# A graph layer with gated mixing: the gate's first layer moves from the prologue into the main loop, and inputs arrive laid out

## The reference

```python
x = x + gnn(xn, edges) + mix(xn)          # 106250 edges, sorted by target
x = x + ffn(layernorm(x))
# gnn: h = xn @ W in 4 heads; softmax over each target's edges of
#      leaky_relu(a_src[src] + a_dst[dst]); sum of alpha * h[src]; + bias; sigmoid
# mix: q, k, v = xn @ Wqkv; context = softmax(k, over nodes)^T v; out = q @ context
#      gate = sigmoid(gelu(ln(xn) @ Wg1 + bg1) @ Wg2 + bg2)     Wg1 is 256 x 64
#      (out * gate) @ Wproj + bproj
# ffn: half of the nodes, the best by a router score, get gelu(y @ w1 + b1) @ w2 + b2
```

## Time and profile before

| | |
|---|---|
| Median of three runs | 1600.1 us (1594.01 to 1605.51) |
| Span of the profiled execution | 1323.1 us |
| The profiled execution's own time | not given; the median is 277.0 us above the span |
| TensorE matmul, weight load busy | 1060.3 us (80%), 791.9 us (60%) |
| VectorE, ScalarE, GpSimd busy | 1018.3 us (77%), 516.7 us (39%), 854.3 us (65%) |
| Mean granted TensorE clock | 0.878 |
| Main block begins at | 136.8 us |

### The profile page before, as it was taken

How to read it: one execution, slowest core, us unless ns; L and a number is a source line. 1 busy time by engine, 2 the same in 40 slices (tenths; PEclk the granted TensorE clock), 3 DMA queues, 4 the chain that set the end, 5 groups by cost and what they waited for, 6 DMA issues and landing times.

```text
span 1323.1 us, 24146 instructions
## 1 busy us (share of the span) xinstructions
PE 1060.3 (80%) x5817; PEld 791.9 (60%) x5817; DVE 1018.3 (77%) x2596; ACT 516.7 (39%) x1155; POOL 854.3 (65%) x891
## 2 busy tenths in 40 slices
PE   5998857785687878878788787897877978779786
PEld 4674635553465566656666566675665766567565
DVE  6776365657788877888788887888878878888788
ACT  4462423212334434343353443434434334344421
POOL 0621656767777777777777777777777777777000
PEclk9999878886788889888898888988889888898889
DMA  9527556766666666666666666666666666665205
GB/s 269 136 72 141 155 184 179 191 178 166 161 173 166 164 160 165 176 158 166 169 162 174 165 161 176 158 171 164 164 173 161 168 164 166 175 164 151 68 1 195
DMA packets 165907, 212.04 MB, mean 160 GB/s; under 512 B 49524, under 2 KB 131252, under 8 KB 165704
## 3 DMA queue, kind: packets, MB, share of 16 engines
q0 software_dynamic: 39984, 110.94, 33.8%
q1 hardware_dynamic: 117570, 97.15, 25.6%
q10 hardware_dynamic: 8306, 3.41, 1.2%
HBM read 165.93 MB, written 45.46 MB: 160 GB/s over the span
## 4 chain that ended last, share of the span: by engine, by line
PE 50%; DVE 15%; issue 11%; ACT 7%; DMA 3%; SPq 1%; DVEq 1%; ACTq 0%; POOL 0%; POOLq 0%
PE bank L1922 15%; PE bank L1887 14%; PE bank L1859 6%; PE bank L1898 5%; ACT L1630 4%; PE bank L1838 3%; DVE hot L1272 2%; PE bank L1847 2%; PE bank L2009 2%; PE bank L1738 2%; DVE ring L1357 2%; DVE xnT L1552 1%; DVE late L1394 1%; DMA parts_d<-wout 1%; ACT bn L1630 1%
## 5 line engine op out<-in xcount | busy, mean ns | idle before, releaser
L774 POOL DMA_INDIRECT ring<-feat_d,idx x832 | 816.0, 981 | 285.8 <-issue 226.5
L1357 DVE TENSOR_TENSOR ring<-ring,bank 128x1024 f32<-128x1024 f32 x208 | 240.0, 1217 | 1.8 <-ACT bank L1620 1.8
L1922 PE MATMUL bank<-late,w_s 128*128 128x256 f32 x768 | 232.4, 463 | 0.4 <-ACT hT L1680 0.4
L1887 PE MATMUL bank<-ring,hot 128*64 128x265 f32 x1664 | 206.8, 401 | 13.3 <-DVE ring L1357 13.2
L1922 PEld LDWEIGHTS bank<-late,w_s 128*128 128x128 f32 x768 | 183.6, 243 | 36.0 <-ACT hT L1680 0.5
L1887 PEld LDWEIGHTS bank<-ring,hot 128*64 128x64 f32 x1664 | 120.0, 141 | 93.8 <-issue 34.2
L1859 PE MATMUL bank<-w_s,hT 128*128 128x256 f32 x720 | 171.0, 392 | 1.2 <-ACT hT L1705 1.2
L1838 PE MATMUL bank<-ident,lk 128*16 128x128 f32 x208 | 42.7, 345 | 161.3 <-DVE lk L1317 161.3
L1620 ACT ACTIVATE bank<-diff 128x64 f32<-128x64 f32 x52 | 11.8, 228 | 376.5 <-DVE diff L1341 362.4
L1859 PEld LDWEIGHTS bank<-w_s,hT 128*128 128x128 f32 x720 | 137.7, 196 | 20.9 <-ACT hT L1705 1.4
L1838 PEld LDWEIGHTS bank<-ident,lk 128*16 128x16 f32 x208 | 17.5, 103 | 177.8 <-DVE lk L1317 136.8
(11 more groups left out here) (284 smaller groups left out, 1611.0 us busy)
## 6 DMA issues: line engine op xcount, KB each, us to landing
parts_d<-zero SPq DMA_DIRECT2D x59, 265.0 KB, 4.0
parts_d<-wout SPq DMA_DIRECT2D x208, 66.2 KB
lists<-dloc_d SPq DMA_DIRECT2D x104, 128.0 KB
ring<-feat_d,idx POOLq DMA_INDIRECT x832
parts<-parts_d SPq DMA_DIRECT2D x49, 265.0 KB
big<-in_x SPq DMA_DIRECT2D x7, 896.0 KB, 11.1
three<-in_x SPq DMA_DIRECT2D x49, 128.0 KB, 3.0
out<-xnT SPq DMA_DIRECT2D x5, 896.0 KB, 4.2
```

What stands on the lines that cost most here:

```text
L774: pool.indirect_dma_start(out=ring[:, u * TI + q, 0:AW], out_offset=None, in_=feat_d, in_offset=bass.IndirectOffsetOnAxis(ap=idx[:, u, q:q ...
L1357: V.tensor_tensor(feats, feats, ex[:, g * TG:(g + 1) * TG, :].unsqueeze(3) .to_broadcast([P, TG, HEADS, HD]), ALU.mult).then_inc(S("scaled ...
L1887: mm = T.matmul(bank[2 + n][c * WIN:(c + 1) * WIN, 0:SW], hot[:, q, :], ring[:, u * TI + q, 0:SW], start=(j == 0), stop=(j == TG - 1))
L1922: mm = T.matmul(bank[6 + g][:, m % 2 * 2 * P:(m % 2 + 1) * 2 * P], w1_s[:, t, m * P:(m + 1) * P], xn2T[:, t, :], start=(t == 0), stop=(t = ...
```

## The change

The host lays the inputs out. `x` comes as 128 rows of 49 x 256 and once more transposed (`xt`), so that `big` and `xnT` are loaded and `turn_pair` and `keep_pair` go. ScalarE issues these 14 loads of 896 KB and eight lists with it; the lists already lie as VectorE and GpSimd use them, so that `turn_lists` and `keep_lists` go. SyncE loads the feature weights first. The joined weight has 264 columns instead of 328, products rotate over four banks instead of two, the 23 key products of the prologue come one per second tile, and ScalarE takes the target column instead of VectorE. The roots are taken in four groups. `Wg1` stays in `wg1_s`. Both inverse deviations come as rows to `rstd_d`. The clears of `parts_d` stand after the last store. In the loop TensorE computes the hidden tile of the gate in `hidden_ahead` (64 x 128, between `other_ff1` and `first_sums`, one step ahead), VectorE scales it (`scale_hidden`, between `outputs` and `products`), and ScalarE applies Gelu (`gate_hidden`, between L1680 and `keep_sums`); `load_scales` takes the place of the load of `hid_d` in SyncE's queue.

```diff
-WA = C + 2 * HEADS + GH
+WA = C + 2 * HEADS
...
+        STOPS = [14, 22, 30, 38]
+        GROUPS = [0, XC, 3 * XC, 5 * XC, NT]
         TARGETS = [0, 26, 42, NT]
+        prod_bank = lambda i: bank[(2, 3, 6, 7)[i % 4]]
+        key_beside = lambda i: i // 2 - 1 if i >= 2 and i % 2 == 0 and i // 2 - 1 < EARLY else None
...
+            feature_weights = [
                 (wa_s[:, :, 0:C], W.rearrange("(t p) n -> p t n", p=P)),
...
+            edge_lists = [
+                (cur_n, curn), (nxt_n, nxtn), (cur_p, curp), (base_p, basep), (cur_t, curt), (nxt_t, nxtt),
+                (first_b, ends[0:1, :].to_broadcast([P, NG])),
+                (srcT[:, :, :].rearrange("p k q -> p (k q)"), srct),
+            ]
+            edge_ends = [(g_first, ends[0:1, :]), (g_last, ends[1:2, :]), (base_i[:, :], first)]
...
+                for p in range(PAIRS):
+                    store(p)
+                    if p == 8:
+                        for o, i in wide:
+                            sp.dma_start(o, i).then_inc(S("weights_in"), 16)
+                    if p == 12:
+                        with nc.allow_non_contiguous_dma(reason="small columns"):
+                            for o, i in columns:
+                                sp.dma_start(o, i).then_inc(S("weights_in"), 16)
+                        sp.wait_ge(S("pool_made"), 7)
+                        sp.dma_start(adst_d[NT * P:ROWS, :], zero[:, 0:SPLIT // 2].bitcast(BF16)).then_inc(S("zeros_out"), 16)
+                for t in (NT, *range(CLEARED)):
+                    clear(t)
...
+                dve.wait_ge(S("features_in"), 16 * len(feature_weights))
+                for n, to in enumerate((xs, sd)):
+                    then(V.tensor_tensor(to, wa_s[:, :, 0:C], sa[:, n, :].unsqueeze(1).to_broadcast([P, CT, C]), ALU.mult))
+                settle()
+                for n, to in enumerate((xs, sd)):
+                    V.tensor_reduce(wa_s[:, :, C + n * HEADS:C + (n + 1) * HEADS],
+                                    to.rearrange("p t (h d) -> p t h d", h=HEADS), AX_X, ALU.add
+                                    ).then_inc(S("weights_ready"), 1)
+                dve.wait_ge(S("columns_summed"), 1)
+                V.scalar_tensor_tensor(wa_s, bank[0][:, 0:WA].unsqueeze(1).to_broadcast([P, CT, WA]), -1.0 / C, wa_s,
+                                       ALU.mult, ALU.add).then_inc(S("weights_ready"), 1)
                 stats(0)
...
-                    V.tensor_scalar(feat_pair[i // 2 % SLOTS][:, i % 2, :], products[:, 0:AW], rstd[:, i:i + 1], None, ALU.mult
+                    V.tensor_scalar(feat_pair[i // 2 % SLOTS][:, i % 2, :], prod_bank(i)[:, 0:AW], rstd[:, i:i + 1], None, ALU.mult
                                     ).then_inc(S("feat_made"), 1)
-                    V.tensor_scalar(adst_s[:, i, :], products[:, AW:AW + HEADS], rstd[:, i:i + 1], None, ALU.mult
-                                    ).then_inc(S("adst_made"), 1)
-                    if i >= 2:
-                        dve.wait_ge(S("hid_made"), i - 1)
-                    V.scalar_tensor_tensor(sc[:, i % 2, 0:GH], products[:, gate_cols], rstd2[:, i:i + 1],
-                                           b1row[:, :], ALU.mult, ALU.add).then_inc(S("hid_asked"), 1)
-                    if 1 <= i <= EARLY:
-                        dve.wait_ge(S("keys_kept"), i)
-                        if i > 1:
-                            dve.wait_ge(S("key_max"), i - 1)
-                        V.tensor_tensor(rmax[:, :], rmax[:, :], big[:, i - 1, :], ALU.max).then_inc(S("key_max"), 1)
+                    j = key_beside(i - 1) if i else None
+                    if j is not None:
+                        dve.wait_ge(S("keys_kept"), j + 1)
+                        if j:
+                            dve.wait_ge(S("key_max"), j)
+                        V.tensor_tensor(rmax[:, :], rmax[:, :], big[:, j, :], ALU.max).then_inc(S("key_max"), 1)
...
+                evacuations(0, 2)
+                stats(1)
+                evacuations(2, 4)
+                stats(2)
+                dve.wait_ge(S("columns_summed"), 3)
+                V.tensor_tensor(b1col[:, :], b1col[:, :], bank[0][0:GH, 0:1], ALU.add)
+                for t in range(CT):
+                    V.tensor_scalar(wg1_s[:, t, :], wg1_s[:, t, :], lng[:, t:t + 1], None, ALU.mult
+                                    ).then_inc(S("weights_ready"), 1)
+                squares(*GROUPS[1:3])
+                evacuations(4, 6)
...
+                for n in range(7):
+                    part = slice(n * XC, (n + 1) * XC)
+                    act.dma_start(xnT[:, part, :], xt[:, part, :]).then_inc(S(f"x{n}_in"), 16)
+                    act.dma_start(big[:, part, :], x[:, part, :]).then_inc(S(f"x{n}_in"), 16)
+                for o, i in edge_lists:
+                    act.dma_start(o, i).then_inc(S("lists_in"), 16)
...
+                    act.wait_ge(S("feat_made"), i + 1)
+                    A.activation(adst_s[:, i, :], prod_bank(i)[:, AW:AW + HEADS], ACT.Copy, scale=rstd[:, i:i + 1]
+                                 ).then_inc(S("adst_made"), 1)
+                    j = key_beside(i)
+                    if j is not None:
+                        act.wait_ge(S("keys_done"), j + 1)
+                        A.activation(big[:, j, :], bank[4 + j % 2][:, 0:C], ACT.Identity, bias=padneg[:, j:j + 1],
+                                     scale=rstd[:, j:j + 1]).then_inc(S("keys_kept"), 1)
...
-                def turn_pair(p):
-                    if p >= 2:
-                        pe.wait_ge(S("xnT_kept"), p - 1)
-                    n = min(2, NT - 2 * p)
-                    pe.wait_ge(S(f"x{(2 * p + n - 1) // XC}_in"), 16)
-                    pe.wait_ge(S(f"x{2 * p // XC}_in"), 16)
-                    for j in range(n):
-                        for t in range(CT):
-                            mm = T.transpose(bank[p % 2][:, (j * CT + t) * P:(j * CT + t + 1) * P],
-                                             big[:, 2 * p + j, t * P:(t + 1) * P], ident[:, :])
...
+                def products(i):
+                    pe.wait_ge(S(f"x{i // XC}_in"), 32)
+                    if i >= 4:
+                        pe.wait_ge(S("adst_made"), i - 3)
                     for t in range(CT):
-                        mm = T.matmul(bank[2 + u][:, 0:WA], tile[:, t * P:(t + 1) * P], wa_s[:, t, :],
+                        mm = T.matmul(prod_bank(i)[:, 0:WA], xnT[:, i, t * P:(t + 1) * P], wa_s[:, t, :],
                                       start=(t == 0), stop=(t == CT - 1))
                     mm.then_inc(S("feat_done"), 1)
-                    if i < EARLY:
-                        if i >= 2:
-                            pe.wait_ge(S("keys_kept"), i - 1)
+                    j = key_beside(i)
+                    if j is not None:
+                        if j == 0:
+                            pe.wait_ge(S("weights_ready"), 4)
+                        if j >= 2:
+                            pe.wait_ge(S("keys_kept"), j - 1)
                         for t in range(CT):
-                            mm = T.matmul(bank[4 + u][:, 0:C], tile[:, t * P:(t + 1) * P], wk_s[:, t, :],
+                            mm = T.matmul(bank[4 + j % 2][:, 0:C], xnT[:, j, t * P:(t + 1) * P], wk_s[:, t, :],
                                           start=(t == 0), stop=(t == CT - 1))
...
+        hid_ps = [bank[2 + n][0:GH, 3 * P:4 * P] for n in range(NB)]
...
-                        sp.wait_ge(S("gate_done"), free)
                     for n in range(2):
                         sp.wait_ge(S(f"window_out{n}"), upto)
                     sp.dma_start(parts[:, u, :, :], parts_d[:, bass.ds(i * P, P), :].rearrange("n p c -> p n c")
                                  ).then_inc(S(f"node_in{u}"), 16)
-                    sp.dma_start(hidT[:, u, :], hid_d[bass.ds(i, 1), :, :].rearrange("a b c -> (a b) c")
-                                 ).then_inc(S(f"node_in{u}"), 16)
+
+                def load_scales(i, u):
+
+                    if not known_below(i, 2):
+                        sp.wait_ge(S("hidT_made"), i - 1)
+                    sp.dma_start(rrow[:, u, :], rstd_d[bass.ds(i, 1), :].to_broadcast([GH, P])
+                                 ).then_inc(S(f"scales_in{u}"), 16)
 
                 def load_x(i, u):
...
+                def scale_hidden(i, u):
+                    dve.wait_ge(S("sums_kept"), NB * (i + LAG_MERGE - 1) + 1)
+                    scale_hidden_from(hid_ps[0], i, u)
+
+                def scale_hidden_from(hid, i, u):
+                    dve.wait_ge(S("hid_done"), i + 1)
+                    dve.wait_ge(S(f"scales_in{u}"), 8 * (i - u) + 16)
+                    V.tensor_tensor(rrow[:, u, :], hid, rrow[:, u, :], ALU.mult).then_inc(S("hid_scaled"), 1)
...
+                def gate_hidden(i, u):
+                    act.wait_ge(S("hid_scaled"), i + 1)
+                    if not known_below(i, 2):
+                        act.wait_ge(S("gate_done"), i - 1)
```

(68 more changed lines are left out.)

436 lines of the change are left out of this document (157 added, 279 removed).

## The result

The change makes the kernel slower: 1634.53 us (median of four, 1630.70 to 1637.80) against 1602.80 (1594.01 to 1609.88), a ratio of 1.0207, 95% interval 1.0163 to 1.0251. In a second set of runs (`after_again`) it was 1618.39 against 1594.28, 1.0159 (1.0141 to 1.0176). Both intervals lie above 1; whether the loss is more than 2% they leave open. The prediction was 1590, with a range up to 1620. The ratios are those on record with their intervals; they differ from the quotients of the medians by up to 0.0032.

The account below looks back on a forecast made before the run. TensorE was taken to pace the prologue; a chain over TensorE, ScalarE and VectorE the loop. 1323.1 - 36 + 25 + 1 = 1313, plus 277.0 above the span, gave 1590 us; range 1563 to 1620.

Parts of the forecast that it names:

- `scale_hidden`'s wait: Loop, VectorE: waits for the row DMA; up to 0.7 us late is covered, beyond is paid; priced at nothing.
- `gate_hidden`'s cover: Loop, ScalarE: 1.8 us of cover before the first copy hides Gelu and table load, 1.6 us; priced at nothing.
- rival 3: Loop: table load ends on the chain because copies come late for another reason; 1590 + 70 = 1660; chance 0.07.
- the sum's first step: Whole kernel: starts from the profiled 1323.1 us and keeps the 277.0 by which the runs' median exceeds the span.
- The prologue, 36 us: Before the loop: less TensorE work starts the main block at 101 instead of 136.8; 36 us gained, ends 24 and 44.
- rival 2: Prologue: ScalarE is held in issuing loads, so the first root comes 28 us later; 1618; chance 0.12.
- `hidden_ahead`, 25 us: Loop, TensorE: added matmuls lie on the chain, 44 x 0.56 = 25 us lost, ends 22 and 44.
- `gate_hidden`'s table load as such: Loop, ScalarE: a table load of 1.28 us, covered, costs nothing; without cover 1.6 x 44 = 70 us.
- The tail, 1 us: Last tiles: two Gelus and a load before the last Ln cost 1 us.
- 1: Rival, loop: added matmuls are hidden because VectorE's scaled rows come later than TensorE; 1600 - 35 = 1565; chance 0.18.
- 4: Rival, loop: the added matmuls run at 1.2 GHz, costing 44 us instead of 25; 1609; chance 0.10.
- 5: Rival, prologue: VectorE and TensorE still wait for each other tile by tile; 20 us gained instead of 36; 1606; chance 0.08.

Follow-up runs that it names:

- after_again: The changed kernel unchanged, timed and profiled again on another chip: 1618.39 us against 1594.28, 1.0159 of the kernel before.
- copies_first: Changed kernel with ScalarE's two copies of the window sums moved ahead of the hidden tile's Gelu and its table load: 0.9959 of the kernel before.
- no_hidden: Changed kernel without the hidden layer's matmuls, scaling, Gelu and row DMA in the loop, hidden tile cleared once: 1567.05 us, 0.9858 of the kernel before.
- spaced: On top of both, ScalarE issues one part of x, waits for small weights and columns, spreads the other loads: 1569.35 us, 0.9835 of the kernel before.
- both: Changed kernel with the row-scale DMA first in SyncE's list and the gate's Gelu in tanh-approximated form: 0.9909 of the kernel before.
- double_hidden: On top of both, each tile's two hidden-layer matmuls issued twice: 1588.03 us, 0.9978 of the kernel before, against 0.9909.
- scales_first: Changed kernel with the row-scale DMA issued first in each step of SyncE's list: 1588.80 us, 0.9997 of the kernel before.
- spaced_exact: Changed kernel with its own Gelu, the row-scale DMA first in SyncE's list and the prologue's loads spaced: 0.9895 of the kernel before.
- run 8: The same run as double_hidden: on top of both, the hidden-layer matmuls issued twice; 1588.03 us, 0.9978 of the kernel before.

## Why the prediction was wrong, point by point

**The step that failed: `scale_hidden`'s wait and `gate_hidden`'s cover**, which the prediction took one by one and set to nothing. It named both covers (0.7 us for the row DMA, "all beyond is paid"; 1.8 us for the table load) and its rival 3 was a table load on the chain. What it missed is that they are coupled: ScalarE's load delays the copies, these delay the window writes ahead of the row DMA in SyncE's queue, and VectorE stands in front of its scans for that DMA. The ring costs what `copies_first` saves: 2.0 to 2.5%, 32 to 40 us, where the prediction had nothing. Without it the change stands at 0.996 of the kernel before, near the forecast's 0.994. That is partly luck: the prologue gained 13 to 20 us less than predicted, and the matmuls cost 14 to 17 less.

**What made it blind to this: the sum's first step**, "1323.1 ... the median of the runs is 277.0 above the span ... I keep it". The 277 us lie inside the span. In the steps from which the covers were read the earlier trace rows, SyncE issued its writes in 4.5 us and nothing was late; in the timed executions a step is 25.97 us, the writes took up to 9.9 us, and a cover of 0.7 us is gone in 26 steps of 49. The prediction doubted this part only in case it moved; a span 17% short of every timed run should have been read as another execution, with every cover doubtful. Whether the ring would cost anything in an execution with steps of 20.8 us no run shows.

**The prologue, 36 us:** 15.6 up to the main block (132.7 to 117.1), 17.3 to the first scan, and 23 (1.4%) in `no_hidden`, which also has the loop's gain from the dropped loads of hidden tiles. Its work was sized well: from first evacuation to last 70.4 us, predicted 72. Its start was not: 36.6 for 18.1. That is rival 2's mechanism (root at 32.8, priced at 42), and beside it the small weights, which landed only at 31.6; the two waits end within 1.2 us of each other, and no run takes them apart. DMA: Bandwidth & Descriptors (section Issuing engines are not separate DMA queues) of the Trainium skill, weighed in rival 2 at 5 us, says that DMAs issued by different engines run on the same 16 DMA engines and interleave. The trace fits it: b1col, issued by 8.6, landed at 31.6, and in `spaced`, with two loads of x ahead of it instead of many, 6.8 us after its issue. With the loads spaced the forecast's picture appears: 21.8, 94.4 and 103.9 for the predicted 18.1, 90 and 101. It is worth 10.5 us in time, with the last evacuation 13.9 earlier (108.3 in `both`).

**`hidden_ahead`, 25 us:** mis-sized: 8 us by the medians, 11 (5 to 17) by the ratios. One tile's records are busy 0.67 us and not 0.56 (33.0 us in 49 tiles of `both`), but by both figures less than half of what `double_hidden` adds reaches the time. So they seem to be on the path in some steps only; in which, and what hides the rest, isn't shown.

**`gate_hidden`'s table load as such:** with the row scales early it costs 0.6 to 0.9% (`both` under `scales_first`, `spaced` under `spaced_exact`, each pair from two chips and with an uncertainty of 0.4 to 0.5), 10 to 14 us of the 56.5 busy; predicted 0. ScalarE: Activation LUTs (section What ACT_TABLE_LOAD costs) of the Trainium skill gives 2.66 us with a drain; the rows again show 1.28 and the Gelu 1.30 us behind its load's start (824.98 to 826.28). That exact and tanh-approximated Gelu are in separate sets, as the prediction took from it (it stands there in the section Table sets: the hidden batching unit), the runs bear out: of the 48 loads on the gate's line 44 are gone with the change of form.

**The tail, 1 us:** 1.3. **The rivals:** 1 had the matmuls cost nothing, and run 8 has 5 to 17 us; but by both figures over half of what was doubled there is hidden, as it says. 4 (44 us) is refuted by the same run. 5 came near in number (15.6 to 17.3 us for its 20) by another cause, since the 70.4 us from first to last evacuation show that the engines did not wait for each other tile by tile. 3 held in kind: the table load reached the chain, through the ring, at 32 to 40 us for its 70. 2 held at 18.5 us for its 28.

## What to carry to other kernels

Check the profile's span against the timed runs before reading any slack from it; a gap of 17% means that the slack of the timed executions is other than shown. When a step puts a wait on a DMA that is queued behind writes whose data come from the same loop, don't price its parts singly: follow once around whether the delayed engine feeds the queue that it waits for. The waits' sum is not the price either: 120.2 us of them were worth 26 to 33, 107.8 in another version some 7. Inputs with no dependence on the step go to the head of the issuing engine's list, table switches behind the copies that others wait for, and bulk loads are issued as they are used, behind the small weights. With all three the changed kernel runs at 0.9899 of the kernel before instead of 1.0159 to 1.0207; without the second it is 0.9895, no different, and with the gate's approximated Gelu in its place 0.9835.

## What the runs showed of the hardware that was not expected

The same program ran with steps of 20.8 us in one execution and 26.0 in another, with the instructions of VectorE and GpSimd as long in both (a scan 1.207 us, a gather 0.98); what differed were spells in which SyncE took up to 868 ns for a register move of 29 ns, with other engines' waits released within 0.9 us of each other at their end, and TensorE's mean granted clock, 0.878 against 0.832. What causes it is open. And an engine that issues large loads is itself held: ScalarE's 22 loads, 0.44 us each at first, took it until 32.8 us, up to 5.47 us for one.
